# Chunked linear attention with a gated FFN on one core: first step with W2 scaled on ScalarE and the FFN products exchanged, state kept as 64x64 blocks

## The reference, cut to what matters

```python
xn = layernorm(x)
q, k, v = silu(xn @ Wq), silu(xn @ Wk), silu(xn @ Wv)          # 16 heads of 16
# per head, with decay ld:  S_t = exp(ld)*S_{t-1} + k_t v_t^T ;  o_t = q_t S_t
o = lightning_attn(q, k, v, log_decay)                          # float32, chunked
gate = (xn @ Wg1) @ Wg2
o = group_rmsnorm(o * sigmoid(gate), 16 heads) * norm_w
s = o @ Wo
# FFN: both operands rounded to float8_e4m3fn
q1 = (xn * scale).astype(FP8);  q2 = (W2 * scale1).astype(FP8)
g = silu((q1 / scale) @ (q2 / scale1))
out = x + s * g
```

## Time and profile before

| | us |
|---|---|
| median of 3 runs | 144.08 |
| lowest and highest of them | 142.39, 145.32 |
| the profiled execution | 140.76 |
| its span, first to last instruction | 139.0 |

### The profile page before, as it was taken

How to read it: one execution, slowest core, us unless ns; L and a number is a source line. 1 busy time by engine, 2 the same in 40 slices (tenths; PEclk the granted TensorE clock), 3 DMA queues, 4 the chain that set the end, 5 groups by cost and what they waited for, 6 DMA issues and landing times.

```text
span 139.0 us, 7207 instructions
## 1 busy us (share of the span) xinstructions
PE 123.4 (89%) x3130; PEld 104.0 (75%) x3130; DVE 103.3 (74%) x276; ACT 75.9 (55%) x143; POOL 72.3 (52%) x112
## 2 busy tenths in 40 slices
PE   3999897945999999999997998999999999887890
PEld 3989895814997799779975896779887987566660
DVE  0899997992888499849990999279937990597963
ACT  7689779829166646664664486365663572104000
POOL 6708999948237186707671584438442842400030
PEclk9999999997799999999999999999999999999999
DMA  2959400000000000100020002000200020020004
GB/s 81 270 155 366 142 0 7 5 0 9 0 0 5 5 5 23 57 5 5 10 73 5 5 0 80 5 5 5 78 5 5 5 78 5 5 80 5 5 0 151
DMA packets 6848, 6.06 MB, mean 44 GB/s; under 512 B 1377, under 2 KB 6817, under 8 KB 6817
## 3 DMA queue, kind: packets, MB, share of 16 engines
q1 hardware_dynamic: 6816, 5.60, 12.6%
HBM read 3.50 MB, written 2.10 MB: 40 GB/s over the span
## 4 chain that ended last, share of the span: by engine, by line
PE 66%; DVE 12%; POOL 10%; issue 8%; ACT 2%; POOLq 0%; DVEq 0%; ACTq 0%
PE b_q L1164 8%; PE b_o L1116 7%; PE b_q L956 5%; PE b_s L1052 4%; PE b_o L1097 4%; PE b_kv L970 4%; PE b_kv L969 4%; PE b_kv L972 4%; PE b_kv L1033 3%; PE b_s L1023 2%; PE b_q L1075 2%; PE b_o L1052 2%; PE b_x L942 2%; PE b_q L961 2%; PE b_s L1006 2%
## 5 line engine op out<-in xcount | busy, mean ns | idle before, releaser
L351 POOL TENSOR_TENSOR e_sum<-e_y,e_magic 128x512 f32<-128x512 f32 x8 | 10.3, 1281 | 19.0 <-DVE e_magic L662 19.0
L710 DVE SCALAR_TENSOR_TENSOR og<-gate_tanh,b_o 128x512 f32<-128x512 f32 x7 | 4.8, 687 | 17.6 <-PE b_o L1116 17.6
L969 PE MATMUL b_kv<-w_hi,xT_hi 128*128 128x256 f32 x64 | 16.6, 281 | 0.0
L970 PE MATMUL b_kv<-w_lo,xT_hi 128*128 128x256 f32 x64 | 16.4, 280 | 0.0
L389 POOL TENSOR_TENSOR y<-sg,x_sb 128x512 f32<-128x512 f32 x7 | 9.0, 1292 | 13.2 <-DVE sg L779 13.2
L1116 PE MATMUL b_o<-probs,v_par 64*32 64x64 f32 x896 | 13.6, 223 | 1.7 <-issue 1.6
L1116 PEld LDWEIGHTS b_o<-probs,v_par 64*32 64x32 f32 x896 | 8.9, 106 | 7.4 <-issue 6.3
L677 DVE TENSOR_TENSOR probs<-b_o,decay_mask 128x512 f32<-128x512 f32 x16 | 10.3, 685 | 4.3 <-PE b_o L1052 4.1
L361 POOL TENSOR_TENSOR qd<-q_silu,q_decay 128x512 f32<-128x512 f32 x8 | 10.4, 1302 | 5.4 <-ACT q_silu L487 5.4
L1164 PE MATMUL b_q<-wo_scaled,on 128*128 128x256 f32 x48 | 13.0, 392 | 0.0
L1052 PE MATMUL b_s<-q_par,kT 32*64 32x128 f32 x256 | 10.1, 293 | 3.1 <-issue 3.1
(11 more groups left out here) (184 smaller groups left out, 353.4 us busy)
## 6 DMA issues: line engine op xcount, KB each, us to landing
out_dram<-y SPq DMA_DIRECT2D x7, 256.0 KB, 2.2
x_sb<-in_L_attn_x_dram SPq DMA_DIRECT2D x4, 384.0 KB, 5.7
x_sb<-in_L_attn_x_dram SPq DMA_DIRECT2D x2, 256.0 KB, 3.5
w_f<-in_L_attn_Wq_dram SPq DMA_DIRECT2D x1, 256.0 KB, 3.6
w_f<-in_L_attn_Wk_dram SPq DMA_DIRECT2D x1, 256.0 KB, 3.8
w_f<-in_L_attn_Wv_dram SPq DMA_DIRECT2D x1, 256.0 KB, 4.7
w_f<-in_L_ffn_input_dram SPq DMA_DIRECT2D x1, 256.0 KB, 3.7
wo_f<-in_L_attn_Wo_dram SPq DMA_DIRECT2D x1, 256.0 KB, 6.1
```

The source lines that it names most:

```text
L351: g.tensor_tensor(e4_sum[:], e4_y[:, n % 2], e4_magic[:, n % 2], ALU.add).then_inc(s_e4sum, 1)
L969: t.matmul(dst[:, s], xT_hi[:, u, kk, tok], w_hi[:, w, kk], start=(s == 0 and kk == 0), stop=False, skip_group_check=True)
L970: t.matmul(dst[:, s], xT_hi[:, u, kk, tok], w_lo[:, w, kk], start=False, stop=False, skip_group_check=True)
```

## The change

Two things are changed.

**The state as 64x64 blocks of four heads.** `state_mid`, `state_end`, `own_mid`, `own_end` and the PSUM views `ps_u` have 64 columns (`C`) for each half and sequence, no longer 32. A matmul of `state_steps` takes 64 columns of `kd` and 64 of v (two pairs of heads), so there are 16 in a step for 32; one of `from_state` takes 64 rows by 64 columns, 8 for each `c` for 16. `own_quad` (128x4) takes the place of `head_parity` in `keep_own`.

**The first step's order.** `w2_y` is made on ScalarE, and the sum of the W2 chain on VectorE, no longer on GpSimd. `head_parity`, `own_block` and `head_sum` are made early on VectorE. GpSimd rounds the first input before it decays the first keys, clears `wg1_a` and `wg1_b` later, and waits for `w2_fp8` (`s_w2q` 6) before `decay_q(1)`. On ScalarE `silu_q_parity(1)` stands ahead of `silu_q(1)`, `silu_v(1)` ahead of `normalise(2)`, and `silu_ffn(1)` ahead of `scale_y(2)` and of `silu_ffn(0)`. On TensorE `ffn(1)` stands ahead of `from_chunk(0, 1, 1)` and `ffn(0)` behind it; the counts of `s_ffn` and `s_ffnps` follow. On VectorE `stats(3)` and `low_xT(2)` stand ahead of `gate_o(0)`.

```diff
-        state_mid = sb("state_mid", [P, PAIRS, KH, S, 2 * E])
+        state_mid = sb("state_mid", [P, PAIRS, KH, S, C])
...
-        ps_u_last = b_x[:, 3 * W // 4:W].rearrange("p (k s e) -> p k s e", k=KH, s=S)
+        ps_u_last = b_x[:, W // 2:W].rearrange("p (k s e) -> p k s e", k=KH, s=S)
...
             def keep_own(dst, src):
-                return g.tensor_tensor(dst.rearrange("p k s (b e) -> p (k s) b e", b=2), src.rearrange("p k s (b e) -> p (k s) b e", b=2),
-                                       head_parity[:].unsqueeze(1).unsqueeze(3).broadcast_to([P, KH * S, 2, E]), ALU.mult)
+                return g.tensor_tensor(dst.rearrange("p k s (h e) -> p (k s) h e", h=4), src.rearrange("p k s (h e) -> p (k s) h e", h=4),
+                                       own_quad[:].unsqueeze(1).unsqueeze(3).broadcast_to([P, KH * S, 4, E]), ALU.mult)
...
-            g.tensor_scalar(w2_y[:], w2_f32[:], scales[:, 1:2], None, ALU.mult).then_inc(s_w2q, 1)
-            decay_k(0)
             sum_y(0)
             round_y(0)
+            decay_k(0)
             decay_q(0)
             norm_factors(2)
-            pool.wait_ge(s_w2q, 3)
-            g.tensor_tensor(w2_m[:], w2_y[:], w2_f32[:], ALU.add).then_inc(s_w2sum, 1)
...
+            pool.wait_ge(s_w2q, 6)
             decay_q(1)
...
             normalise(1)
+            act.wait_ge(s_w2, 16)
+            act.wait_ge(s_scale[1], 16)
+            a.activation(w2_y[:], w2_f32[:], ACT.Copy, scale=scales[:, 1:2]).then_inc(s_w2q, 1)
             silu_q(0)
...
             put_nan(1)
+            stats(3)
+            low_xT(2)
             gate_o(0)
-            low_xT(2)
...
                 if n > 0:
-                    pe.wait_ge(s_ffn, n + 1 if n < STEPS - 1 else n)
+                    pe.wait_ge(s_ffn, 1 if n == 1 else n + 1 if n < STEPS - 1 else n)
...
                     for s in range(S):
-                        for r in range(4):
+                        for quad in range(2):
                             for c in range(2 if pos(n) < NB - 1 else 1):
...
-                                mm = t.matmul(u_ps[c][32 * r:32 * r + 32, half, s], kd[rows, u, s, half * P + 32 * r:half * P + 32 * r + 32],
-                                              heads[:, s * HH + half * 4 + r, :, 0:E], start=True, stop=True, skip_group_check=True)
+                                first = s * HH + half * 4 + 2 * quad
+                                mm = t.matmul(u_ps[c][C * quad:C * quad + C, half, s], kd[rows, u, s, half * P + C * quad:half * P + C * quad + C],
+                                              heads[:, first:first + 2, :, 0:E], start=True, stop=True, skip_group_check=True)
...
-                        for r in range(4):
-                            rows = slice(32 * r, 32 * r + 32)
+                        for quad in range(2):
+                            rows = slice(C * quad, C * quad + C)
```

More of the change, by code:

```diff
@@ L162, in layer_kernel @@
         ps_ffn0 = b_q[:].rearrange("p (s n) -> p s n", s=S)
-        ps_u = [b[:, 0:W // 4].rearrange("p (k s e) -> p k s e", k=KH, s=S) for b in (b_q, b_k)]
+        ps_u = [b[:, 0:W // 2].rearrange("p (k s e) -> p k s e", k=KH, s=S) for b in (b_q, b_k)]
         ps_k = b_k[:].rearrange("p (s n) -> p s n", s=S)
@@ L584, in _ @@
             high_g1(0)
+            act.wait_ge(s_wg2, 64)
+            a.activation(wg2_hi[:], wg2_f32[:], ACT.Copy).then_inc(s_g2w, 1)
             scale_y(1)
             find_over(0)
+            act.wait_ge(s_qps, 2)
+            silu_q_parity(1)
             silu_q(1)
-            silu_q_parity(1)
             silu_k(1)
+            silu_v(1)
             normalise(2)
-            silu_v(1)
             gate(0)
@@ L599, in _ @@
             high_xT(2)
+            act.wait_ge(s_dvec, 4)
+            silu_ffn(1)
             scale_y(2)
-            act.wait_ge(s_dvec, 6)
+            square_o(0)
             silu_ffn(0)
-            square_o(0)
-            silu_ffn(1)
             act.wait_ge(s_wo, 48)
@@ L665, in put_nan @@
                 dve.wait_ge(s_over, n + 1)
-                need(dve, s_ffnps, n - 1)
+                need(dve, s_ffnps, n - 1 if n != 2 else 2)
                 v.scalar_tensor_tensor(out=xqT[:, n % 2].rearrange("p k t -> p (k t)"), in0=ps_over, scalar=0.0, in1=e4_q[:],
@@ L799, in _ @@
             v.tensor_scalar(not_ahead[:], lag[:], 0.0, None, ALU.is_ge).then_inc(s_ahead, 1)
+            dve.wait_ge(s_pool, 12)
+            for half in range(KH):
+                hs = v.tensor_scalar(head_sum[:, half].rearrange("p (j z) -> p j z", j=8)[:, :, half * HH:half * HH + HH],
+                                     own_head[:].unsqueeze(1).broadcast_to([P, 8, HH]), 0.5, None, ALU.mult)
+            hs.then_inc(s_hsum, 1)
             dve.wait_ge(s_w[0], 16)
@@ L839, in _ @@
                 mask(0, r)
+            dve.wait_ge(s_w2q, 1)
+            v.tensor_scalar(w2_m[:].bitcast(I32), w2_y[:].bitcast(I32), 0x7F800000, None, ALU.bitwise_and).then_inc(s_w2q, 1)
             low_xT(1)
@@ L849, in _ @@
             magic(1)
[L850 to L851 removed]
             dve.wait_ge(s_w2q, 2)
             v.tensor_scalar(w2_f32[:], w2_m[:], E4_MIN, E4_MAGIC, ALU.max, ALU.mult).then_inc(s_w2q, 1)
+            dve.wait_ge(s_w2q, 3)
+            v.tensor_tensor(w2_m[:], w2_y[:], w2_f32[:], ALU.add).then_inc(s_w2sum, 1)
             put_nan(0)
@@ L860, in _ @@
             v.reciprocal(inv_scales[:], scales[:]).then_inc(s_dvec, 1)
-            for half in range(KH):
-                hs = v.tensor_scalar(head_sum[:, half].rearrange("p (j z) -> p j z", j=8)[:, :, half * HH:half * HH + HH],
-                                     own_head[:].unsqueeze(1).broadcast_to([P, 8, HH]), 0.5, None, ALU.mult)
-            hs.then_inc(s_hsum, 1)
-            dve.wait_ge(s_dvec, 5)
+            dve.wait_ge(s_dvec, 3)
             v.tensor_scalar(descale[:], inv_scales[:, 0:1], inv_scales[:, 1:2], None, ALU.mult).then_inc(s_dvec, 1)
@@ L1217, in _ @@
             from_state(0, 1)
+            pe.wait_ge(s_w2q, 6)
+            ffn(1)
             from_chunk(0, 1, 1)
+            ffn(0)
             pe.wait_ge(s_hsum, 1)
@@ L1222, in _ @@
             mm.then_inc(s_pec, 1)
-            pe.wait_ge(s_w2q, 6)
-            ffn(0)
-            ffn(1)
             for n in range(1, STEPS - 1):
```

54 lines of the change are left out of this document (26 added, 28 removed).

## The result

The changed kernel took 133.59 us (median of 4 runs, 133.10 to 134.09), the kernel before, run beside it, 143.24 us (4 runs, 141.56 to 145.32): 0.941 of the time, 95% interval 0.932 to 0.950. The forecast was 135.4, with a range of 131.5 to 140.5. The profiled executions took 133.10 and 140.76 us, spans 131.4 and 139.0. A median is taken over all runs of a kernel, a ratio only over those within 1.5% of its fastest run.

The account below looks back on a forecast made before the run. TensorE's own queue was taken as the bound in the middle steps, beside a 3.13 us stand before `scores(1)`. Terms 3.4 + 1.5 + 0.7 + 2.0 + 1.1 = 8.7 us, from the median 144.08, gave 135.4; range 131.5 to 140.5.

Parts of the forecast that it names:

- a stall of a packet's length in another place: Sign of being wrong: TensorE stalls as long as those for instruction packets, in other places than before.
- `state_steps` at 0.5 to 0.6: Sign of being right: the state matmuls of a step last 0.5 to 0.6 us, against 0.69 before.
- middle steps at 13.9: Sign of being right: middle steps last 13.9 us with no stall inside a run of small matmuls.
- Part 1: First step's new order: `scores(1)` starts at 29.5 and not 32.94, gaining 3.4 us; bounds 0.8 to 3.9.
- GpSimd is held until `w_fp8` is done: First step: the hold keeps GpSimd's `qd` from running beside VectorE's 1.69 us `w_fp8`, taking 1.0 from VectorE's queue.
- Part 2: Step after `scores(1)`: TensorE keeps its full clock, 13.5 us and not 15.04, gaining 1.5; bounds 0 to 1.7.
- Part 3: 64x64 state blocks: `state_steps` gains 0.12 us in each of six steps, 0.7 in all; `from_state` gains nothing.
- 8 rounds of 58 ns and the same 0.1: 0.57: New `state_steps`: 32 passes on four tiles, plus 0.1 for the change of tile form, take 0.57 us.
- halving the count halves what runs side by side: `from_state` gains nothing: its blocks go from four 32x32 tiles to two 64x64, each still with 4 matmuls.
- Rival 3: State matmuls: 64-column weight loads are not hidden, so the kernel gets slower, 151 us; chance 0.04.
- Part 4: Fewer TensorE instructions end stalls for instruction packets: 2.0 us in two middle steps, 1.1 in the last, 3.1 in all.
- a loss if edges fall badly: Bound on the gain from instruction packets: badly placed packet edges could cost one more such stall, 1.0 us.

Follow-up runs that it names:

- the blocks alone: The kernel before with only the 64x64 state blocks, in the first step's old order: 139.16 us, ratio 0.981 to the kernel before.
- the order alone: The changed kernel with the old 32-column state blocks put back, so only the first step's new order: 138.04 us, ratio 0.964 to the kernel before.
- the changed kernel's repeat: The changed kernel run once more, nothing changed, beside the runs with more TensorE instructions at the start: 134.05 us.
- no hold: The changed kernel without GpSimd's wait for `w2_fp8` ahead of `decay_q(1)`: 133.11 us, ratio 0.939 to the kernel before.

## Why the prediction was right

The direction, the size and the mechanism of the larger parts held; two of the five terms did not (the blocks, and the stalls of the last step). Balance on the profiled executions: 7.7 us measured, 8.7 worked out. The medians fell by 9.65, more than either. That the sum came so near is in part luck: parts 3 and 4 were 1.5 us too high together and part 1 was 0.7 too low. Of the prediction's own signs of being wrong one came, a stall of a packet's length in another place (117.42), and of its signs of being right `state_steps` at 0.5 to 0.6 and middle steps at 13.9 did not.

- **Part 1, first step, 3.4 us: 4.07 measured, mechanism right but for one step.** The start was put at 29.5 and came at 28.87; 4.07 is also more than the 3.9 that the prediction called the most there could be, for that bound counted two waits and not the masks. All the way it ran 0.5 to 0.7 ahead of the working: `find_over(1)` ended at 25.94 and not near 26.5. The term left out is W2's scaling beside VectorE: with it on GpSimd `e_exp(0)` and `e_magic(0)` take 0.82 and 0.86, without it 0.43 each, and the masks start 0.8 earlier. The run with W2 back on GpSimd shows it alone: 29.70 with it, 28.87 without. Wrong was the step "GpSimd is held until `w_fp8` is done": `w_fp8` is as fast without the hold, because it now comes before `qd` begins. What moved it ahead of `qd` is the earlier queue of VectorE. Of the 4.07, the FFN exchange alone is worth 31.10 - 28.87 = 2.2, less some 0.4 from the start of that run, and the place of W2 0.8; the rest, some 1.0 to 1.4, was not split further.
- **Part 2, clock, 1.5 us: 1.39 measured.** The row is 1.00 and the step 13.65, and undoing the FFN exchange brings back 0.89 and 14.95. It also shows part 1 and part 2 as one event: a stand of TensorE of 2.86 or 3.13 us ahead of `scores(1)` was followed by the low clock in each of the three traces that have one, the changed kernel's longest there, 0.5, was not.
- **Part 3, blocks, 0.7 us: about nothing.** The failed step is "8 rounds of 58 ns and the same 0.1: 0.57". `state_steps` measured 0.63, so the change of tile form or the rounds cost more than the guess (66 ns a round, if the 0.1 stands), and `from_state` 1.08 in place of 1.03. Middle steps of 14.00 to 14.02 us stand against 14.04 and 13.95: zero within what they vary. The step that was right is the one beside it, "halving the count halves what runs side by side". Rival 3 did not come: 64-column weights did not show. The 32 passes of `from_state` took 34 ns each on two row groups, 68 ns for each group, though one load lasts 134 to 135 ns; that is against the rule of the Trainium skill ("TensorE: Matmul & The Clock Gate", Part 3) on loads and row groups, as the chunk products had been. VectorE and GpSimd took their doubled columns at no cost in the new order (`keep_own` 613 ns in place of 458); in the old one they cost 0.5 us ahead of `scores(1)`.
- **Part 4, packets, 3.1 us: 2.3 measured.** In the middle 1.16 + 0.89 - 0.23 = 1.8 for 2.0; the blocks alone show the same with no other edit, and the order alone shows the long stalls without them. In the last step 0.5 for 1.1: a stall of 1.06 stands where 0.68 and 0.42 stood. The failed step is to take the last step's stalls as gone because the dense part has fewer instructions. It is still dense there, and an edge still falls into it. The 0.68 was under-priced as well: with it gone the last masks start 1.06 us sooner, which is where the 0.5 comes from, the new stall taking back the rest. The bound "a loss if edges fall badly" is what happened, in part.
- **The median.** It was worked out by adding 3.3 us to the profiled time. The kernel before runs 141.6 to 145.3, the changed one 133.1 to 134.1, so the changed kernel also lost the spread. The granted clock goes with it: of the 29 runs of the kernel before that stood beside the experiments, the twelve at 0.984 to 0.988 took 140.4 to 143.3 us, the six at 0.959 to 0.965 took 144.1 to 146.2, and the others lie between in clock and overlap both in time (141.1 to 144.3), while the four runs of the changed kernel all had 1.00. So in an average run more clock is probably saved than in the profiled one, and the forecast was 1.8 too high.

Open: why stalls of 1.06, 1.27, 0.57 and 0.84 us stand at the same edge in different executions, and whether the low clocks of the kernel before all come from the stand before `scores(1)` or in part from packet stalls, as in the order alone. Both were seen, neither was counted. How long a packet takes to come, and why, no run here shows.

## What to carry to other kernels

Where TensorE is the bound and its queue holds runs of hundreds of small matmuls, look for idle time that no semaphore ends, count the instructions between such places, and if they are a packet apart, take instructions out of the dense run or move the edge; do not expect it from the arithmetic. Price a stand of TensorE with the clock behind it, which here cost from half of the wait (1.4 us after 3.13) to more than the wait again (1.8 after 1.53), or nothing (after 1.08). And halving the number of matmuls by doubling their columns gains nothing where they already ran on twice as many tiles side by side (1.08 us for 1.03).

## What the runs showed of the hardware that I had not expected

- Stalls for instructions stand 256 TensorE instructions or a multiple apart, as near as the records can tell: in the order alone one ends at 70.95 and one at 82.87, with 252 matmuls and 252 weight loads between, two stalls of the changed kernel's repeat end at 115.39 and 119.37 with 129 and 129, and 64 or 192 more instructions at the start moved the last one by 59 to 65 records (a few are missing from each trace).
- Such a stall can be followed by the low clock as well: behind one of 1.53 us four matmuls took 1.64 us in place of 0.86.
- Small matmuls can be cheap when they change tiles. 72 passes on one 128x32 tile took 2.77 us (38 ns each, 23 ns in its later part), 72 passes on sixteen 32x32 tiles 0.83 us (11 ns each). The size of the tile changed with their number, so which of the two it is remains open. The chain of the first and the window of the second:

```profile
5.90 2.77 PE b_s L1189 x72
```

```profile
5.70:6.53 0.83, 0.82 (x73) 0.69 (x72) 0.74 (x3) 0.69 (x4) 0.47 (x4) 1.00 0.85 256
```

- VectorE operations of 0.43 us took 0.82 and 0.86 beside a GpSimd operation on 128x512 f32 (`w_y`; the run with W2 back on GpSimd), but `w_fp8` took 0.87 beside `own_end` of GpSimd (128x256, no hold) and 1.69 beside `qd` (128x512, the kernel before).
